# Last layer of a gated graph network: the order of h minus n, the row statistics and the moment operations on the vector engine

## The chip, the cores and the metric

The kernel runs on one core of one Trainium2 chip. The metric is the device time of one execution in microseconds (us), the median over runs. The engines are TensorE (PE in the profile), VectorE (DVE), ScalarE (ACT), GpSimd (POOL) and SyncE (SP), which here only issues transfers.

## The reference

50,000 nodes with 128 features each go through four layers of a gated graph convolution, then through a residual sum and a layer normalisation over each row. The graph has 75,000 directed edges (25,000 drawn ones and a loop on every node).

```
for l in range(4):
    m = x @ weight[l]
    agg = segment_sum(m[src], dst)
    gi = agg @ w_ih.T + b_ih ;  gh = x @ w_hh.T + b_hh      # three parts each: r, z, n
    r = sigmoid(i_r + h_r) ;  z = sigmoid(i_z + h_z) ;  n = tanh(i_n + r * h_n)
    x = (1 - z) * n + z * x                                 # = n + z * (x - n)
y = x + 2 * node_embed
out = (y - mean(y)) / sqrt(var(y) + 1e-5)                   # by row
```

## The kernel before

The nodes are cut into 100 blocks of 500. A block is held transposed, 128 features by 500 nodes, and products are split into high and low parts for precision. Each layer is a loop over blocks in which every engine has its own instruction stream in a hand-written order; waits on semaphores tie the streams together. The loop body is unrolled over ten blocks (`UNROLL`), so a position `u` runs from 0 to 9, and buffers are used in rings of five (`RING`).

In step b of a layer the vector engine does, for block b unless another is named:

- `r_times_hn` (L1363): `narg` = (h_n + bias) * r. It waits for `rg`, the sigmoid that ScalarE makes (L1055).
- `renew` = `new_state` of block b-1 (L1389).
- `n_argument` (L1370): adds the i_n product. ScalarE's tanh (L1059) waits for it.
- `aggregate` of block b+2 (L1344). ScalarE's rounding to the high part `a_hi` (L1042) waits for it.
- last layer only: `remainder` = `residual` of block b-2 (L1398), then `row_stats` of block b-2 (L1405): four batch-norm statistics instructions of 128 columns that read the rows that the residual has just written, behind a wait for it (L1403).
- `difference` (L1374): h minus n, behind a wait for the tanh.
- `low_part` of block b+2 (L1335).
- `product` (L1380): z times the difference. TensorE's next z product and GpSimd's next low part of h wait for it.

Small operations on 125 x 20 values normalise five blocks at once, in two positions of each ten. `half` is set at u = 2 and 7: there `moments` (three operations, L1410 to L1412) stands ahead of `difference`, `squared_difference` (L1416) behind it, and `variance` (L1422) behind `product`. The moments read the statistics of blocks b-7 to b-3, finished a step before. GpSimd's `root` (L658) waits for the variance at u = 3 and 8, and at u = 4 and 9 `shift` (L1428) on the vector engine waits for the root and stands between `r_times_hn` and the new state.

ScalarE's order in a step of the last layer is: `rg` (L1055), high part of h (L1025), first half of the output rows of block b-9 (L1077), tanh, `a_hi` of block b+2, z gate (L1063), widening of the selection (L1037), second half of the output rows, and then `rg` of the next step.

GpSimd's order is: low part of h (L652) for block b+3, `root` where there is one, and three gathers (L675) for block b+5. SyncE loads and stores in an order of its own; its load of columns for block b+5 waits for `difference`, and its load of x rows waits for the residual.

Of the kernel before, what the change touches and what calls it, by code (L numbers as in the profile page):

```python
# [31 lines left out]
RING = 5  # L32
# [17 lines left out]
ROWLAG = 2  # L50
# [25 lines left out]
def build(nc, x, src, dst, weight, w_ih, w_hh, b_ih, b_hh, out):  # L76
# [26 lines left out]
    with ctx:  # L103
# [264 lines left out]
        def after(i, u, k=1):  # L368

            i, u = i + (u + k) // UNROLL, (u + k) % UNROLL  # L370
            return UNROLL * i + u, u, i
# [10 lines left out]
        def halved(l):  # L382

            return 0 < l < L - 1
# [29 lines left out]
        def half_done(i, u, at):  # L414

            if u % RING != at % RING:
                return None
            first = u - at
            hi, hu = i + first // UNROLL, first % UNROLL
            if isinstance(hi, int) and hi < 0:  # L420
                return None
            return slice(hu, hu + RING), turn(hi, hu)
# [765 lines left out]
        def _(dve):  # L1188
# [170 lines left out]
            def r_times_hn(l, b, u):  # L1359
                g = l * NB + b  # L1360
                dve.wait_ge(s_HN, g + 1)
                dve.wait_ge(s_r, g + 1)
                v.scalar_tensor_tensor(narg[:, :], pHN[:, 0:COLS], bhh[:, 2:3], rg[:, :],  # L1363
                                       ALU.add, ALU.mult).then_inc(s_t1, 1)
# [66 lines left out]
            def fast_path():  # L1431
                for l in range(L):
                    final = l == L - 1

                    def renew(b, u, i):

                        g = l * NB + b
                        t = turn(i, u)
                        again = not (isinstance(t, int) and t == 0 and l == 0)
                        new_state(l, b, u, (TURNS * l + t if not final else TURNS * l) if again else None,  # L1440
                                  g - RING + 1 if again else None)

                    def remainder(b, u, i):
                        later = not (isinstance(i, int) and i == 0)
                        residual(b, u, u % RING, TURNS + turn(i, u) + 1, l * NB + b - UNROLL + 1 if later else None)

                    def step(i, u, first, last):
                        b = UNROLL * i + u
                        if first:
                            if l == 0:  # L1450
                                for j in range(TILES):
                                    select(1, 1, j)
                            first_aggregate(l, 0, l == 0)
                            first_low_part(l, 0)
                            first_aggregate(l, 1, l == 0)
                            first_low_part(l, 1)
                            first_aggregate(l, 2, l == 0)
                            first_low_part(l, 2)
                            if l == 0:
                                for c in range(2, RAMP):  # L1460
                                    for j in range(TILES):
                                        select(c, c, j)

                        added = final and exists_before(i, u, ROWLAG)
                        half = half_done(i, u, RING + ROWLAG) if final else None
                        shifted = half_done(i, u, OUTLAG) if final else None
                        ramp = isinstance(i, int) and i == 0 and u < RAMP
                        if last:
                            renew(*after(i, u, -1))
                        if ramp and u:  # L1470
                            renew(*after(i, u, -1))
                        if ramp and u == 3:
                            aggregate(l, 4, 4)
                        r_times_hn(l, b, u)
                        if shifted:
                            shift(*shifted)
                        if not ramp and not last:
                            renew(*after(i, u, -1))
                        n_argument(l, b, u)
                        if ramp and u == 3:  # L1480
                            low_part(l, 4, 4)
                        summed = after(i, u, 1 if ramp else 2)[:2] if exists(i, u, 2) else None
                        if summed and not (ramp and u == 3):
                            aggregate(l, *summed)
                        if added and not ramp:
                            remainder(*after(i, u, -ROWLAG))
                            row_stats(*after(i, u, -ROWLAG)[:2])
                        if half:
                            moments(*half, RING * (half[1] + 1))
                        if l == 0 and exists(i, u, RAMP) and not ramp:  # L1490
                            for j in range(TILES):
                                select(*after(i, u, RAMP)[:2], j)
                        difference(l, b, u)
                        if half:
                            squared_difference(*half)
                        if not opening(i) and exists(i, u, 3) and not final:
                            low_gathered(l, *after(i, u, 3)[:2])
                        coming = on_from(l, i, u, PRE)
                        coming = coming if coming and halved(coming[0]) else None
                        if coming and not ramp and not last:  # L1500
                            low_h(*coming[:3])
                        if summed and not (ramp and u == 3):
                            low_part(l, *summed)
                        if ramp and u == 3:
                            aggregate(l, 5, 5)
                        product(l, b, u)
                        if coming and ramp:
                            low_h(*coming[:3])
                        if half:
                            variance(*half)  # L1510
                        if ramp and u == 3:
                            low_part(l, 5, 5)
                        if opening(i) and not unsplit(l, b + 3):
                            low_gathered(l, *after(i, u, 3)[:2])
                        if added and ramp:
                            remainder(*after(i, u, -ROWLAG))
                            row_stats(*after(i, u, -ROWLAG)[:2])
                        if l == 0 and ramp:
                            for j in range(TILES):
                                select(RAMP + u, RAMP + u, j)  # L1520
                        if last:
                            renew(b, u, i)
                            if coming:
                                low_h(*coming[:3])

                    blocks(dve, step)
                    if final:
                        def last_rows(k):
                            u = UNROLL - k

                            dve.wait_ge(s_nmr, turn(GROUPS - 1, u) + (1 if k > LATE else 2))
                            for c in range(RPP // 2, RPP):
                                row = y_rows[:, u, c * D:(c + 1) * D]
                                last = v.tensor_scalar(row, row, rstd[:, u, c:c + 1], nmr[:, u, c:c + 1], ALU.mult, ALU.add)
                            last.then_inc(s_olast, 1)

                        ahead = slice(RING, UNROLL - LATE), TURNS - 1
                        late = slice(UNROLL - LATE, UNROLL), TURNS
                        moments(*ahead, NB - LATE)
                        squared_difference(*ahead)  # L1540
                        variance(*ahead)
                        for k in range(LATE, 0, -1):
                            remainder(NB - k, UNROLL - k, GROUPS - 1)
                            row_stats(NB - k, UNROLL - k)
                        shift(*ahead)
                        moments(*late, NB)
                        squared_difference(*late)
                        variance(*late)
                        for k in range(RING, LATE, -1):
                            last_rows(k)  # L1550
                        shift(*late)
                        for k in range(LATE, 0, -1):
                            last_rows(k)
# [79 lines left out]
```

## Time and profile before

| | us |
|---|---|
| median of 3 runs | 2382.85 (2382.22 to 2384.59) |
| the profiled execution, its own time | 2379.24 |
| its span, first to last instruction | 2377.3 |
| DVE busy over the span | 2185.7 (92%) |
| PE busy | 2251.5 (95%) |
| ACT busy | 1846.3 (78%) |
| POOL busy | 1747.0 (73%), a gather takes 1.04 in the mean |

All times below are of the one profiled execution. A step of the last layer is a stretch from one `r_times_hn` to the next. Instructions on VectorE and ScalarE overlap in the records: the next one starts a little before the end of the one ahead, so what a step consists of is the distances from start to start, not the durations.

### The profile page before, as it was taken

The page shows a single profiled execution, that of the slowest core. Times are in us where ns is not written, and L with a number is a line of the kernel's source. Part 1 is how long each engine was busy: PE and PEld are TensorE (multiplying, and loading weights), DVE is VectorE, ACT ScalarE, POOL GpSimd, SP SyncE. Part 2 cuts the span into 40 slices and gives each one's busy share as a digit, 9 for nine tenths or more (in the row PEclk, how much of TensorE's full clock was granted, in tenths as well). Part 3 has the DMA queues.
Part 4 walks back from the last instruction along what each step waited for, and adds up shares of the span by engine and source line. Part 5 has one row for each costly group of instructions (what it writes and reads, how often), then busy time and mean ns, then how long its engine had stood idle before and what let it go on. Part 6 is the DMA issues. An engine that isn't in the chain of part 4 may idle for free.

```text
span 2377.3 us, 49608 instructions
## 1 busy us (share of the span) xinstructions
PE 2251.5 (95%) x11728; PEld 1904.3 (80%) x11728; DVE 2185.7 (92%) x4408; ACT 1846.3 (78%) x3483; POOL 1747.0 (73%) x1654
## 2 busy tenths in 40 slices
PE   3899999999989999999979999999989999999996
PEld 2788888888868888888868888888877877777885
DVE  7699999999869999999959999999969999999998
ACT  1588888888758888888847888888856888888887
POOL 3778888888477777777647777777747888888884
PEclk7899999999999999999989999999999999999998
DMA  2355555555535555555535555555543555555553
GB/s 57 98 154 161 160 157 159 159 161 157 151 110 167 171 167 170 171 172 169 170 100 168 172 171 167 172 166 172 171 140 101 155 155 159 153 152 156 157 156 116
DMA packets 277063, 362.44 MB, mean 152 GB/s; under 512 B 107754, under 2 KB 186586, under 8 KB 276980
## 3 DMA queue, kind: packets, MB, share of 16 engines
q1 hardware_dynamic: 238196, 309.20, 42.5%
q0 software_dynamic: 38784, 52.30, 9.6%
q8 instruction: 32, 0.52, 0.1%
q14 instruction: 51, 0.42, 0.1%
HBM read 208.71 MB, written 179.20 MB: 163 GB/s over the span
## 4 chain that ended last, share of the span: by engine, by line
PE 65%; DVE 18%; issue 10%; ACT 4%; another core or an unknown queue 1%; DMA 1%; DVEq 1%; ACTq 0%; POOL 0%; SPq 0%; POOLq 0%
PE pR L839 17%; PE pZ L839 17%; PE pHN L839 8%; PE pA L827 8%; PE pO L906 6%; PE pIN L839 4%; PE pA L839 4%; DVE bn L1405 3%; DVE aggT L1344 2%; DVE diff L1374 2%; DVE y_rows L1398 2%; DVE diff L1380 2%; PE pH L778 2%; DVE narg L1370 1%
## 5 line engine op out<-in xcount | busy, mean ns | idle before, releaser
L675 POOL DMA_INDIRECT gath<-state,idx x900 | 933.3, 1037 | 266.4 <-issue 255.6
L652 POOL TENSOR_TENSOR h_lo<-hT,h_hi 128x500 fp32r<-128x500 f32 (+1 forms) x400 | 376.1, 940 | 220.7 <-ACT h_hi L1025 115.0
L675 POOL DMA_INDIRECT gath<-in_x_dram,idx x300 | 347.5, 1158 | 102.3 <-issue 74.8
L1055 ACT ACTIVATE rg<-pR,bsum 128x500 f32<-128x500 f32 x400 | 269.7, 674 | 132.5 <-PE pR L839 61.2
L1363 DVE SCALAR_TENSOR_TENSOR narg<-pHN,bhh,rg 128x500 f32<-128x500 f32 x400 | 294.0, 735 | 62.9 <-ACT rg L1055 31.1
L1380 DVE TENSOR_TENSOR diff<-pZ,diff 128x500 f32<-128x500 f32 x400 | 269.0, 672 | 9.6 <-ACT pZ L1063 6.7
L1344 DVE TENSOR_TENSOR aggT<-pA,hT 128x500 f32<-128x500 f32 x396 | 265.8, 671 | 8.5 <-remote 4.9
L1335 DVE TENSOR_TENSOR a_lo<-aggT,a_hi 128x500 fp32r<-128x500 f32 x396 | 271.2, 685 | 0.8
L1037 ACT CAST sel<-sel 128x504 fp32r (+1 forms) x400 | 245.6, 615 | 30.2 <-DVE flag_i L1319 29.8
L1063 ACT ACTIVATE pZ<-pZ,bsum 128x500 f32<-128x500 f32 x400 | 256.3, 641 | 10.6 <-remote 10.4
L906 PEld LDWEIGHTS pO<-ident,newT 128*125 128x125 f32 x1400 | 202.5, 187 | 55.0 <-DVE newT L1389 16.4
L1042 ACT CAST a_hi<-aggT 128x500 fp32r<-128x500 f32 x396 | 235.8, 596 | 12.0 <-DVE aggT L1344 7.0
L1059 ACT ACTIVATE pIN<-narg,bih 128x500 f32<-128x500 f32 x200 | 136.5, 683 | 130.9 <-DVE narg L1370 79.2
L1059 ACT ACTIVATE pA<-narg,bih 128x500 f32<-128x500 f32 x200 | 136.5, 682 | 130.2 <-DVE narg L1370 71.0
L906 PE MATMUL pO<-ident,newT 128*125 128x128 f32 x1400 | 214.3, 276 | 15.3 <-DVE newT L1389 13.8
L839 PE MATMUL pZ<-a_hi,wf_hi 128*128 128x500 f32 x400 | 184.0, 460 | 15.4 <-issue 8.2
L827 PE MATMUL pA<-sel,g_lo 128*128 128x168 f32 x810 | 194.8, 275 | 0.0
L839 PE MATMUL pR<-h_hi,whh_hi 128*128 128x500 f32 x400 | 190.8, 477 | 2.7 <-ACT rg L1055 2.7
L827 PE MATMUL pA<-sel,g_hi 128*128 128x168 f32 x810 | 186.3, 264 | 1.1 <-issue 0.8
L1069 ACT COPY o_rows<-pO 125x512 f32<-125x512 f32 x300 | 175.8, 586 | 7.1 <-PE pO L906 7.1
L1025 ACT CAST h_hi<-hT 128x500 fp32r<-128x500 f32 x300 | 179.9, 600 | 0.0
L839 PE MATMUL pR<-a_hi,wf_hi 128*128 128x500 f32 x400 | 159.2, 398 | 17.1 <-DVE a_lo L1335 9.9
(205 smaller groups left out, 6404.0 us busy)
## 6 DMA issues: line engine op xcount, KB each, us to landing
columns<-newT SPq DMA_DIRECT2D x300, 250.0 KB
hT<-columns SPq DMA_DIRECT2D x300, 250.0 KB
state<-o_rows SPq DMA_DIRECT2D x300, 224.0 KB
x_rows<-in_x_dram SPq DMA_DIRECT2D x200, 224.0 KB
out_dram<-o_rows SPq DMA_DIRECT2D x91, 224.0 KB
gath<-state,idx POOLq DMA_INDIRECT x900
state<-o_rows SPq DMA_DIRECT2D x300, 26.0 KB
idx<-edge_src SPq DMA_DIRECT2D x395, 1.5 KB
```

Of the source, the lines that this page charges most:

```text
L652: nc.gpsimd.tensor_tensor(part_of(h_lo, u)[:, cols], hT[:, u % RING, cols], part_of(h_hi, u)[:, cols].bitcast(F32), ALU.subtract).then_inc ...
L675: pool.indirect_dma_start(out=gath[:, u % RING, j, :], out_offset=None, in_=states[l], in_offset=bass.IndirectOffsetOnAxis(ap=idx[:, u % R ...
L827: last = nc.tensor.matmul(to, rows, cols, start=begins, stop=ends)
L839: last = nc.tensor.matmul(bank, w, xx, start=begins and k == 0, stop=ends and k == len(passes) - 1)
L906: last = nc.tensor.transpose(bank[0:ROWS, k * D:(k + 1) * D], newT[:, u % RING, k * CP:k * CP + ROWS], ident[:, :])
L1055: nc.scalar.activation(rg[:, :], pR[:, 0:COLS], ACT.Sigmoid, bias=bsum[:, 0:1]).then_inc(s_r, 1)
L1059: nc.scalar.activation(n_bank(u), narg[:, :], ACT.Tanh, bias=bih[:, 2:3]).then_inc(s_n, 1)
L1063: nc.scalar.activation(pZ[:, 0:COLS], pZ[:, 0:COLS], ACT.Sigmoid, bias=bsum[:, 1:2]).then_inc(s_z, 1)
L1335: v.tensor_tensor(by_rows(a_lo[:, u % RING, :]), sums_of if summed else by_rows(aggT[:, :]), by_rows(a_hi[:, u % RING, :].bitcast(F32)), A ...
L1344: v.tensor_tensor(by_rows(aggT[:, :]), sums_of, by_rows(hT[:, u % RING, :]), ALU.add).then_inc(s_agg, 1)
L1363: v.scalar_tensor_tensor(narg[:, :], pHN[:, 0:COLS], bhh[:, 2:3], rg[:, :], ALU.add, ALU.mult).then_inc(s_t1, 1)
L1380: v.tensor_tensor(diff[:, :], pZ[:, 0:COLS], diff[:, :], ALU.mult).then_inc(s_e, 1)
```

## The change

Three things move in the last layer's steps; no operation is added or taken away. `difference` goes ahead of `row_stats`, directly behind `residual`. `moments` goes behind `low_part`, ahead of `product`; `squared_difference` goes behind `product`. `variance` goes into the next step, behind its `r_times_hn`, ahead of the new state.

```
+                        spread_out = half_done(i, u, RING + ROWLAG + 1) if final else None
 ...
                         r_times_hn(l, b, u)
+                        if spread_out:
+                            variance(*spread_out)
                         if shifted:
                             shift(*shifted)
 ...
                             remainder(*after(i, u, -ROWLAG))
-                            row_stats(*after(i, u, -ROWLAG)[:2])
-                        if half:
-                            moments(*half, RING * (half[1] + 1))
 ...
                         difference(l, b, u)
-                        if half:
-                            squared_difference(*half)
+                        if added and not ramp:
+                            row_stats(*after(i, u, -ROWLAG)[:2])
 ...
+                        if half:
+                            moments(*half, RING * (half[1] + 1))
                         product(l, b, u)
+                        if half:
+                            squared_difference(*half)
                         if coming and ramp:
                             low_h(*coming[:3])
-                        if half:
-                            variance(*half)
```

## Rows read from the trace of the kernel before

**Rows 1.** Windows, last layer: us, then busy us by engine (instructions), PE clock, DMA share, GB/s.
```profile
1850.00:2300.00 450.00, 439.58 (x2171) 359.15 (x2169) 447.34 (x1025) 381.64 (x775) 388.34 (x325) 1.00 0.54 155
```
**Rows 2.** Timeline, VectorE, one ordinary step: start, us, engine, line, operation, tiles.
```profile
2106.06 0.74 DVE L1363 SCALAR_TENSOR_TENSOR narg<-pHN,bhh,rg 128x500 f32<-128x500 f32 x1
...
2107.30 0.67 DVE L1370 TENSOR_TENSOR narg<-pIN,narg 128x500 f32<-128x500 f32 x1
2107.89 0.67 DVE L1344 TENSOR_TENSOR aggT<-pA,hT 128x500 f32<-128x500 f32 x1
2108.47 0.68 DVE L1398 SCALAR_TENSOR_TENSOR y_rows<-x_rows,pO 125x512 f32<-125x512 f32 x1
2109.19 0.87 DVE L1405 BATCH_NORM_STATS2 bn<-y_rows 125x6 f32<-125x128 f32 x4
2109.97 0.66 DVE L1374 TENSOR_TENSOR diff<-hT,pIN 128x500 f32<-128x500 f32 x1
2110.55 0.68 DVE L1335 TENSOR_TENSOR a_lo<-aggT,a_hi 128x500 fp32r<-128x500 f32 x1
2111.14 0.67 DVE L1380 TENSOR_TENSOR diff<-pZ,diff 128x500 f32<-128x500 f32 x1
2111.76 0.74 DVE L1363 SCALAR_TENSOR_TENSOR narg<-pHN,bhh,rg 128x500 f32<-128x500 f32 x1
```
**Rows 3.** Timeline, ScalarE, the same step.
```profile
2108.01 0.68 ACT L1059 ACTIVATE pIN<-narg,bih 128x500 f32<-128x500 f32 x1 [0.77 <-issue]
2108.62 0.60 ACT L1042 CAST a_hi<-aggT 128x500 fp32r<-128x500 f32 x1
2109.13 0.64 ACT L1063 ACTIVATE pZ<-pZ,bsum 128x500 f32<-128x500 f32 x1
...
2110.20 0.88 ACT L1077 ACTIVATE o_rows<-y_rows,nmr,rstd 125x128 f32<-125x128 f32 x2
2110.98 0.66 ACT L1055 ACTIVATE rg<-pR,bsum 128x500 f32<-128x500 f32 x1
```
**Rows 4.** Timeline, VectorE, two early steps without output rows on ScalarE.
```profile
1808.20 0.73 DVE L1363 SCALAR_TENSOR_TENSOR narg<-pHN,bhh,rg 128x500 f32<-128x500 f32 x1
...
1813.86 0.73 DVE L1363 SCALAR_TENSOR_TENSOR narg<-pHN,bhh,rg 128x500 f32<-128x500 f32 x1
```
**Rows 5.** Timeline, VectorE, the step with `half`, which starts at 2111.76.
```profile
2115.67 0.18 DVE L1410 TENSOR_TENSOR mv<-bn 125x20 f32<-125x20 f32 x1
...
2115.97 0.67 DVE L1374 TENSOR_TENSOR diff<-hT,pA 128x500 f32<-128x500 f32 x1
...
2117.84 0.19 DVE L1422 SCALAR_TENSOR_TENSOR veps<-mv 125x20 f32<-125x20 f32 x1
2117.94 0.73 DVE L1363 SCALAR_TENSOR_TENSOR narg<-pHN,bhh,rg 128x500 f32<-128x500 f32 x1
```
**Rows 6.** Timeline, ScalarE, the `rg` that ends in that step.
```profile
2116.68 0.66 ACT L1055 ACTIVATE rg<-pR,bsum 128x500 f32<-128x500 f32 x1
```
**Rows 7.** Timeline, VectorE, the shift ahead of the new state.
```profile
2124.29 0.18 DVE L1428 SCALAR_TENSOR_TENSOR nmr<-mv,rstd 125x20 f32<-125x20 f32 x1
2124.38 0.66 DVE L1389 TENSOR_TENSOR newT<-diff,pIN 128x500 f32<-128x500 f32 x1
```
**Rows 8.** Timeline, GpSimd: the first root, a later root, and two gathers behind it.
```profile
1829.15 3.58 POOL L658 TENSOR_TENSOR rstd<-veps,mhalf 125x20 f32<-125x20 f32 x1
...
2119.53 3.57 POOL L658 TENSOR_TENSOR rstd<-veps,mhalf 125x20 f32<-125x20 f32 x1
...
2124.65 1.00 POOL L675 DMA_INDIRECT gath<-state,idx  x1 [0.31 <-issue]
...
2128.42 1.36 POOL L675 DMA_INDIRECT gath<-state,idx  x1 [0.16 <-issue]
```
**Rows 9.** Waits, 1850 to 2300: who waited for whom: us in total, times, longest.
```profile
POOL gath L675 <- issue: 57.9, 225, 0.3
PEld pZ L839 <- issue: 25.7, 62, 0.8
```

## The prediction

> **What bounds the kernel now.** I read the page first, then the last layer by windows, and then one step of it engine by engine in the timeline. From 1850 to 2300 us VectorE is busy 447 of 450 us at a granted TensorE clock of 1.00 [rows 1]. That looks as if every 0.01 us saved on VectorE came off the time. The timeline of a step says otherwise.
>
> An ordinary step runs from one r times h_n to the next, 2106.06 to 2111.76, 5.70 us [rows 2]. All distances from start to start between long VectorE operations are 0.58 or 0.59, with two exceptions. One is residual to row statistics, 2108.47 to 2109.19, 0.72. The other is product to the next r times h_n, 2111.14 to 2111.76, 0.62. The second shows a wait: rg starts at 2110.98 and ends at 2111.64 [rows 3], and r times h_n starts 0.12 later. In the step with the small operations rg ends at 2117.34 [rows 6] and r times h_n starts 0.60 after it [rows 5], so there VectorE's own order was last. In the ordinary steps ScalarE was.
>
> So there is a loop over two engines, and it sets an ordinary step:
>
> - VectorE, r times h_n to aggregate (the new state and the n argument between): 2106.06 to 2107.89, 1.83, and the aggregate's 0.67 [rows 2]: 2.50
> - its end at 2108.56 to the start of a_hi at 2108.62: 0.06 [rows 3]
> - ScalarE without a pause: a_hi to z gate 0.51, z gate to output rows (the widening between) 1.07, output rows to rg 0.78, rg itself 0.66 [rows 3]: 3.02
> - rg to r times h_n: 0.12
>
> The sum is 5.70, the step as measured. VectorE's own order, had nothing held it, is 5.70 less the 0.03 by which the product's distance (0.62) exceeds the usual 0.59: 5.67. The early steps agree. There ScalarE has no output rows, and a step is 1813.86 - 1808.20 = 5.66 [rows 4]. VectorE and the loop lie 0.03 apart, and the loop is the longer.
>
> TensorE is not the bound: in those 450 us (79 steps of 5.70, or 77 with the longer ones) it waited 25.7 us ahead of the z product in the weight loads alone [rows 9], a third of a us per step. GpSimd is close: 388.3 us busy [rows 1] and 57.9 us between gathers [rows 9] are 446 of 450.
>
> **Ordinary steps, three of five.** The difference moves between the residual and the row statistics. The statistics' wait for the residual is then satisfied when they come up, and their distance falls from 0.72 to 0.59: 0.13 saved. No row shows statistics behind a difference. The bounds are 0 saved (the distance stays whatever stands ahead) and 0.15 (0.57, just under the shortest distance between long operations in this step); I take 0.13, since every long pair in the step without a fresh result has 0.58 or 0.59. VectorE's own order becomes 5.54. But statistics, difference, low part and product are none of them in the loop, which stays 5.70. What is late next is rg, as now; r times h_n then waits 0.16 longer. Value: 0. If that cover were gone (a loop as short as VectorE's order), it would be worth 0.13 per step.
>
> The difference itself comes earlier. It would start at 2108.47 + 0.59 = 2109.06; the tanh ends at 2108.69 [rows 3], 0.37 before, and rg shows 0.12 to be enough from a ScalarE end to a VectorE start. 0.25 is left. Cost 0. Queued behind it are the statistics, the low part and the product, all with slack. SyncE's load of columns waits for the difference and goes 0.9 us earlier in its queue, ahead of an output store that waits for ScalarE; the DMA share is 0.54 [rows 1], so I give it nothing.
>
> **The step with half, one in five.** It is 2117.94 - 2111.76 = 6.18 now [rows 2, 5], which is VectorE's own order: 5.67 and five small operations of about 0.10 (three moments take 0.30 from 2115.67 to 2115.97, the variance 0.10 from 2117.84 to 2117.94). The moments were already waiting for nothing new, and so was the squared difference behind a whole h minus n; the new places save no stall there. After the change: 6.18 less 0.13 for the statistics, less 0.10 for the variance that leaves the step: 5.95. That is still above the loop's 5.70, so VectorE is last and the whole 0.23 comes off the time.
>
> **The step behind it.** The variance now stands between r times h_n and the new state, inside the loop. The nearest row is the shift in the same place, 2124.29 to the new state at 2124.38: 0.09 [rows 7]; I take 0.10, the distance the variance has today; bounds 0 and 0.19, its whole duration. The step goes from 5.70 to 5.80. The step with the shift keeps its 5.79 or so.
>
> GpSimd's root waits for the variance. Now the variance ends at 2118.03 and the root starts at 2119.53 [rows 8], behind the low part of h. After, it ends at 2117.94 - 0.23 + 0.66 + 0.19 = 2118.56, with 0.97 to spare. The root ends at 2123.10 and the shift runs at 2124.29, 1.19 later. Cost 0; without that cover, each us would hold up the shift and with it the new state.
>
> **The sum.** Per five blocks: -0.23 + 0.10 = -0.13. There are 19 such groups in the steps; in the first, the root at 1829.15 to 1832.73 [rows 8] ends a moment before its shift and is behind GpSimd's gathers, so I give that group nothing. 18 x 0.13 = 2.3 us. Profiled execution: 2379.24 - 2.3 = 2376.9. The median of the runs is 3.6 above it; the same difference on the median gives 2380.5. Layers 0 to 2, the ramp and the tail behind the last step keep their order and get 0. From the bounds: 0.15 and 0 for variance give -0.25 per group, -4.5 us; 0 and 0.19 give +0.09, +1.6.
>
> A rule speaks against the step that earns this. The Trainium skill, page "VectorE: DVE Perf Modes", section "The DRAIN you can't avoid", says that chained VectorE operations took the same time with a semaphore after each as with one at the end: the semaphore costs nothing extra. The row has 0.72 against 0.59, so I take the row. By the rule the 0.13 would stay, and the sum would be 18 x (0.10 - 0.10) = 0.
>
> **The rivals.**
>
> (a) Nothing comes of it: the 0.72 belongs to the statistics, not to the wait. For it: only this one pair shows 0.72, and its first operation differs in kind from all others. Against it: the start 0.03 behind the residual's end, where all other pairs overlap. The group's sum is 0: 2382.85. The skill's rule above is this case.
>
> (b) All steps gain. The 0.12 from rg to r times h_n would be chance and VectorE the only bound. For it: 447 of 450 us busy. Against it: the same 0.12 in ordinary steps, 0.60 in the step with small operations, and 5.66 where ScalarE has less to do. Price: 0.13 x 96 blocks = 12.5 us. But GpSimd doesn't follow so far: five steps take 3 x 5.70 + 6.18 + 5.79 = 29.07 now, and the slack I can see is the one gather of 1.36 against 1.00 or so [rows 8], some 0.35. 19 x 0.35 = 6.7: 2376.2, or 2370.4 if GpSimd gives way.
>
> (c) Slower: GpSimd becomes the bound. It is occupied 446 of 450 us and has its one long gather where the low part of a step begins. The low part moves 0.13 earlier in the step, and a second gather of the fifteen per group could meet it. That is +0.35 per group on 29.07. It decides from the group in which the root's spare 1.19 is used up: 1.19 / (0.35 + 0.13), after two or three groups. 16 x 0.35 = 5.6: 2388.5. Against it: why that gather is long isn't shown, and in five steps only one is.
>
> (d) The tanh comes too late for the earlier difference. It would have to end 0.25 + 0.16 = 0.41 later than now. It has 0.77 of idle time ahead of it and starts right behind its argument. I give it little; it is in the remainder.
>
> **How the numbers follow.** Forecast 0.68, (a) 0.12, (b) 0.08, (c) 0.07, the rest 0.05, on both sides. About 0.2%, 4.8 us, is what a measurement can tell from no change. The forecast and (a) are within it. Faster by more: (b) and some of the rest, and the edge of the forecast: 0.13. Slower by more: (c) and a little: 0.07. The same: 0.80. The range from 2376.5 to 2384.6 holds the forecast with its bounds, (a) with the spread of the runs, and leaves out most of (b) and (c). The forecast's own range is 2378.3 to 2382.5.
>
> **What would show it.** Ordinary steps still 5.69 to 5.70, with rg ending 0.12 before r times h_n and product to r times h_n now about 0.75. Residual to difference and difference to statistics 0.59 each. Step with half about 5.95, the next about 5.79, 28.9 per five. A step of 5.6 or less would refute the loop. Statistics 0.72 behind the difference would confirm (a). A shift that starts right behind the root's end in every group would mean (c).

## The result, and the profile after

The changed kernel takes 2396.53 us (six runs, 2390.53 to 2398.44) against 2384.01 us for the kernel before (2382.22 to 2387.55): a ratio of 1.0043, 95% interval 1.0031 to 1.0055. By that ratio, of runs taken in turn, it is slower by about 10 us; the two medians lie 12.5 apart. The forecast was 2380.5, a little faster, with a range up to 2384.6.

The profiled execution took 2396.49 us, its span is 2394.6. All that was moved did what it should, except for one instruction, the variance. Here is VectorE's timeline of a step with half and the step behind it, in the changed kernel; it answers to [rows 2, 5].

```profile
1979.60 0.68 DVE L1398 SCALAR_TENSOR_TENSOR y_rows<-x_rows,pO 125x512 f32<-125x512 f32 x1
1980.20 0.67 DVE L1374 TENSOR_TENSOR diff<-hT,pIN 128x500 f32<-128x500 f32 x1
1980.78 0.87 DVE L1405 BATCH_NORM_STATS2 bn<-y_rows 125x6 f32<-125x128 f32 x4
...
1983.04 0.19 DVE L1416 SCALAR_TENSOR_TENSOR mv<-mv 125x20 f32<-125x20 f32 x1
1983.14 0.74 DVE L1363 SCALAR_TENSOR_TENSOR narg<-pHN,bhh,rg 128x500 f32<-128x500 f32 x1
1983.79 0.80 DVE L1422 SCALAR_TENSOR_TENSOR veps<-mv 125x20 f32<-125x20 f32 x1
1984.51 0.66 DVE L1389 TENSOR_TENSOR newT<-diff,pIN 128x500 f32<-128x500 f32 x1
...
1989.54 0.74 DVE L1363 SCALAR_TENSOR_TENSOR narg<-pHN,bhh,rg 128x500 f32<-128x500 f32 x1
```

Residual to difference is 0.60 and difference to statistics 0.58: the 0.72 of [rows 2] is gone. The step with half starts at 1977.19 (the row is in the fence after next) and ends at 1983.14: 5.95, as forecast. But the variance takes 0.80 instead of the 0.19 of [rows 5], the new state starts 0.72 behind it, and the step is 1989.54 - 1983.14 = 6.40 instead of 5.80. GpSimd's timeline at that moment shows what it ran beside:

```profile
1982.18 1.25 POOL L675 DMA_INDIRECT gath<-state,idx  x1 [0.30 <-issue]
1983.44 1.08 POOL L652 TENSOR_TENSOR h_lo<-hT,h_hi 128x500 fp32r<-128x500 f32 x1
1984.67 3.57 POOL L658 TENSOR_TENSOR rstd<-veps,mhalf 125x20 f32<-125x20 f32 x1
```

The low part of h runs from 1983.44 to 1984.52. The variance comes up at 1983.79, inside it, and ends at 1984.59, 0.07 behind its end. Only then does the new state go on, and it lies in the loop. Below, an instruction is called held when its record is longer than the same operation's elsewhere and ends with an instruction of the other engine.

The ordinary steps are 5.69, as before. VectorE and ScalarE around one of them:

```profile
1971.50 0.74 DVE L1363 SCALAR_TENSOR_TENSOR narg<-pHN,bhh,rg 128x500 f32<-128x500 f32 x1
...
1976.45 0.67 DVE L1380 TENSOR_TENSOR diff<-pZ,diff 128x500 f32<-128x500 f32 x1
1977.19 0.74 DVE L1363 SCALAR_TENSOR_TENSOR narg<-pHN,bhh,rg 128x500 f32<-128x500 f32 x1
```
```profile
1976.42 0.66 ACT L1055 ACTIVATE rg<-pR,bsum 128x500 f32<-128x500 f32 x1
```

Product to r times h_n is now 0.74, and r times h_n still starts 0.11 behind rg's end at 1977.08. VectorE gained 0.13 per step and spends it waiting for ScalarE.

Over steps 10 to 89 of the last layer (the ten first and last ones left out) five blocks take, from the starts of r times h_n in each trace, 29.05 us before and 29.51 after. 18 groups make 18 x 0.46 = 8.3 us of the 10. The spans of the two profiled executions differ by more, 17.3 us: 3.9 of it has come about before the last layer's first step, where no instruction was moved, and 5.1 in the first ten steps (71.4 against 66.3); experiment 12 looks at these.

### The profile page after: what moved, and what is told of

It reads as the page before. It is cut to its first block, busy times and chain, and to the rows that moved or that the text cites. A ratio compares the mean times of both kernels' runs of the same rounds, so it can differ in the third digit from the quotient of the medians.

```text
span 2394.6 us, 49608 instructions
## 1 busy us (share of the span) xinstructions
PE 2254.5 (94%) x11728; PEld 1900.1 (79%) x11728; DVE 2189.0 (91%) x4408; ACT 1846.3 (77%) x3483; POOL 1753.7 (73%) x1654
## 4 chain that ended last, share of the span: by engine, by line
PE 65%; DVE 19%; issue 8%; ACT 4%; another core or an unknown queue 2%; DMA 1%; DVEq 1%; POOL 0%; SPq 0%; ACTq 0%; POOLq 0%
PE pR L839 17%; PE pZ L839 16%; PE pHN L839 8%; PE pA L827 8%; PE pO L906 5%; PE pA L839 4%; PE pIN L839 4%; DVE narg L1370 3%; DVE diff L1374 2%; DVE bn L1405 2%; DVE aggT L1344 2%; DVE a_lo L1335 2%; DVE diff L1380 2%; PE pH L778 2%
## 5 line engine op out<-in xcount | busy, mean ns | idle before, releaser
L1335 DVE TENSOR_TENSOR a_lo<-aggT,a_hi 128x500 fp32r<-128x500 f32 x396 | 269.3, 680 | 0.7
```

Source lines behind the costliest of these rows:

```text
L1335: v.tensor_tensor(by_rows(a_lo[:, u % RING, :]), sums_of if summed else by_rows(aggT[:, :]), by_rows(a_hi[:, u % RING, :].bitcast(F32)), A ...
```

## The experiments

Each was timed in turn with the kernel before on one chip, and its ratio is to that. "Per five" is the mean of the sixteen groups of steps 10 to 89. The steps are those of one typical group; u is the position in a ring of five. In 2, 3, 6, 10, 11 and 12 one or two groups of the sixteen differ from it, in 3 and 12 one with a step of 7.36, which raises their mean by 0.06.

| | ratio (95%) | per five | the steps u = 0 to 4 |
|---|---|---|---|
| before | | 29.05 | 5.69, 5.69, 6.19, 5.69, 5.79 |
| changed | 1.0043 (1.0031 to 1.0055) | 29.51 | 5.69, 5.69, 5.95, 6.40, 5.79 |
| 1 swap only | 0.9985 (0.9973 to 0.9997) | 28.94 | 5.67, 5.69, 6.07, 5.68, 5.83 |
| 2 variance only | 1.0065 (1.0049 to 1.0081) | 29.77 | 5.69, 5.69, 6.09, 6.49, 5.79 |
| 3 one input | 1.0026 (1.0012 to 1.0039) | 29.56 | 5.69, 5.69, 5.95, 6.38, 5.79 |
| 4 spread | 1.0038 (1.0025 to 1.0052) | 29.70 | 5.67, 5.85, 5.74, 5.69, 6.75 |
| 5 root first | 1.0036 (1.0023 to 1.0048) | 29.61 | 5.67, 5.69, 5.96, 5.79, 6.48 |
| 6 variance later | 1.0045 (1.0031 to 1.0059) | 29.61 | 5.67, 5.69, 5.96, 6.18, 6.12 |
| 7 output rows together | 0.9991 (0.9979 to 1.0003) | 28.93 | 5.65, 5.65, 6.18, 5.67, 5.78 |
| 8 swap, rows together | 0.998 (0.9966 to 0.9993) | 28.90 | 5.53, 5.53, 6.13, 5.53, 6.16 |
| 9 PSUM input | 0.9989 (0.9979 to 1.0) | 28.91 | 5.69, 5.69, 5.95, 5.79, 5.79 |
| 10 all moved | 1.0029 (1.0018 to 1.0041) | 29.54 | 5.53, 5.85, 5.74, 6.34, 6.09 |
| 11 cheap root | 0.9957 (0.9941 to 0.9973) | 28.32 | 5.53, 5.85, 5.74, 5.63, 5.53 |
| 12 changed again | 1.004 (1.0027 to 1.0054) | 29.56 | 5.69, 5.69, 5.95, 6.39, 5.78 |

**1. Swap only.**

```
                             remainder(*after(i, u, -ROWLAG))
-                            row_stats(*after(i, u, -ROWLAG)[:2])
...
                         difference(l, b, u)
                         if half:
                             squared_difference(*half)
+                        if added and not ramp:
+                            row_stats(*after(i, u, -ROWLAG)[:2])
```

> Only the difference and the row statistics change places; moments, squared difference and variance stay where they were before. Theory P (the variance met GpSimd's low part of h in the step behind the half): nothing stalls here. Ordinary steps 5.69 to 5.70, half step 6.18 - 0.13 = 6.05, the next 5.69, so -0.13 per five blocks, some 2.3 us faster than before (0.1%). Rival Q (the early difference or the later statistics cost the time): the step behind the half or the ordinary steps stay longer than before and the kernel is slower, up to the 10 to 12 us of the whole change.

The half step is 6.07, the next 5.68: the swap by itself makes the kernel faster, by 0.11 per five blocks and 0.15% in the runs. The early difference costs nothing. The rival falls.

**2. Variance only.** What experiment 1 leaves out of the change, less the moves of the moments and the squared difference:

```
                         r_times_hn(l, b, u)
+                        if spread_out:
+                            variance(*spread_out)
...
                         product(l, b, u)
...
-                        if half:
-                            variance(*half)
```

> Only the variance moves, from behind the product into the next step, between r times h_n and the new state; all else as before. Theory P: the variance lasts 0.8 us or more instead of 0.19, since it starts inside GpSimd's low part of h and ends with it; the half step is 6.08, the next 6.4, about +0.6 per five blocks, +10 us (0.4 to 0.5% slower). Rival Q: half step 6.08 and next 5.79, sum as before, within 0.1%.

All the loss is here, and more than all: 6.09 and 6.49, +0.72 per five blocks. The variance takes 0.90 and ends with the low part:

```profile
2003.86 0.90 DVE L1422 SCALAR_TENSOR_TENSOR veps<-mv 125x20 f32<-125x20 f32 x1
```
```profile
2003.62 1.08 POOL L652 TENSOR_TENSOR h_lo<-hT,h_hi 128x500 fp32r<-128x500 f32 x1
```

The low part's end is 2004.70, the variance's 2004.76.

**3. One input.** The changed kernel with a variance that reads one tensor (it leaves the squared difference out, so the output differs):

```
-                v.scalar_tensor_tensor(veps[:, s, :], mv[:, s, :, 1], 1.0 / D, mv[:, s, :, 3],
-                                       ALU.mult, ALU.add).then_inc(s_eps, 1)
+                v.tensor_scalar(veps[:, s, :], mv[:, s, :, 1], 1.0 / D, EPS, ALU.mult, ALU.add).then_inc(s_eps, 1)
```

> The changed kernel, but the variance reads one tensor (the within-half variance) and two constants; the squared difference of the half means is left out of it, so the output differs. Theory P in the form that the stall needs a VectorE instruction with two SBUF tensor inputs: the variance takes 0.2 us, the step behind the half 5.79, five blocks 28.9, 2 to 3 us faster than before. Rival R (any small VectorE operation at that place stalls, for instance on its wait for the squared difference 0.75 us earlier, or on GpSimd whatever it reads): the step stays at 6.4 and the kernel 10 us slower than before.

The narrower form of the theory falls: with a single SBUF input the instruction still takes 0.78 and the step 6.38.

```profile
2006.39 0.78 DVE L1422 TENSOR_SCALAR veps<-mv 125x20 f32<-125x20 f32 x1
```

Its low part ran from 2006.04 to 2007.13.

**9. PSUM input.** Run later, but it is the counterpart: the same place, and the second tensor lies in PSUM (the values differ, and the second operation is a maximum instead of a sum). The added lines make L1428 the variance's line in this kernel.

```
+                v.scalar_tensor_tensor(veps[:, s, :], mv[:, s, :, 1], 1.0 / D,
+                                       n_bank(u)[0:ROWS, 0:RING * RPP].rearrange("p (r k) -> p r k", k=RPP),
+                                       ALU.mult, ALU.max).then_inc(s_eps, 1)
```

> The changed kernel, but the second tensor that the variance reads lies in PSUM (twenty columns of the tanh result) instead of SBUF, so its value is another and the output differs. In the traces so far no VectorE operation with a PSUM operand was lengthened beside GpSimd's low part, while operations with all tensors in SBUF were, even with one input. If that is the line, the variance takes 0.2 us, the step behind the half 5.79 and five blocks 28.9 to 29.2 (a later low part of the sums may still be held). If any small operation is held, 0.8 us and 6.40 again.

It takes 0.18 to 0.19, and in the early groups it does so inside a low part. VectorE and GpSimd in two of them:

```profile
1896.04 0.19 DVE L1428 SCALAR_TENSOR_TENSOR veps<-mv,pA 125x20 f32<-125x20 f32 x1
1925.01 0.18 DVE L1428 SCALAR_TENSOR_TENSOR veps<-mv,pIN 125x20 f32<-125x20 f32 x1
```
```profile
1895.70 1.08 POOL L652 TENSOR_TENSOR h_lo<-hT,h_hi 128x500 fp32r<-128x500 f32 x1
...
1924.66 1.08 POOL L652 TENSOR_TENSOR h_lo<-hT,h_hi 128x500 fp32r<-128x500 f32 x1
```

1896.04 lies 0.34 behind the low part's start, as the held variance of the changed kernel does (0.35), and it is not lengthened. From the sixth group on, the variance starts 0.01 to 0.05 ahead of the low part, so only the first five are the test. The step behind the half is 5.79 and five blocks take 28.91: the sum of the prediction, had the variance not been held.

**4. Spread.** The swap, and the small operations spread over two steps, out of the loop (the lines against the kernel before; the variance stays where it was there):

```
+                        if early:
+                            moments(*early, RING * (early[1] + 1))
+                        if half:
+                            squared_difference(*half)
                         product(l, b, u)
```

> The swap, and the small operations over two steps: moments one step earlier, between low part and product; the squared difference in the half step between low part and product; the variance behind the product as before. None of them stands between r times h_n and aggregate. From the loop of 5.70 and VectorE's own order of 5.54 in a step: 5.84 with the three moments, 5.74 with the squared difference and variance, then 5.70, 5.79 (shift) and 5.70, so 28.77 per five blocks against 29.07: 19 x 0.30 = 5.5 us faster than before (0.2%). If VectorE alone were the bound, ordinary steps would be 5.54 and the gain over 10 us. If the low parts or the small operations meet GpSimd's work in their new places, single steps exceed these values by up to 0.8 us.

Four of five steps are as worked out, 5.85, 5.74, 5.69 and 5.67. The step with the shift is 6.75. There the low part of the sums (`low_part`, L1335), on VectorE, meets the low part of h, on GpSimd:

```profile
2013.19 1.75 DVE L1335 TENSOR_TENSOR a_lo<-aggT,a_hi 128x500 fp32r<-128x500 f32 x1
```
```profile
2013.13 1.26 POOL L652 TENSOR_TENSOR h_lo<-hT,h_hi 128x500 fp32r<-128x500 f32 x1
```

1.75 is 1.10 more than its 0.65. A long operation is held as a short one is: it ends 0.55 behind the low part of h, nearly its whole own duration, as if it began only there.

**5. Root first.** The changed kernel; GpSimd's root ahead of its low part:

```
...
+                        if half:
+                            root(*half)
                         coming = on_from(l, i, u, PRE)
                         if coming:
                             split_h(*coming[:3], l * NB + b if exists_before(i, u, 1) else None)
...
-                        if half:
-                            root(*half)
```

> The changed kernel, but on GpSimd the root stands ahead of the low part of h in the steps u = 3 and 8, so no low part can run when the variance comes. Theory H (a VectorE operation whose tensors all lie in SBUF, other than the row statistics, is held while GpSimd's low part runs): the variance takes 0.2 us instead of 0.8 and the step behind the half 5.79 instead of 6.40. The low part moves to about 5 us behind r times h_n, where it can meet the next low part of the sums; then one later step is up to 0.8 us longer than in the changed kernel, and the sum stays open between 28.9 and 29.7 per five blocks. Rival R (the variance is slow at that place by itself, for instance by its wait for the squared difference): 0.8 us and 6.40 as before, whatever GpSimd does.

The variance takes 0.18 and the step 5.79. Nothing on VectorE was touched, so the place alone isn't slow, nor is the wait for the squared difference. The next low part of h lands on the low part of the sums, which takes 1.51 in the step with the shift, and 6.48 follows: the loss is paid elsewhere.

```profile
1999.10 0.18 DVE L1422 SCALAR_TENSOR_TENSOR veps<-mv 125x20 f32<-125x20 f32 x1
...
2008.70 1.51 DVE L1335 TENSOR_TENSOR a_lo<-aggT,a_hi 128x500 fp32r<-128x500 f32 x1
```
```profile
2008.38 1.28 POOL L652 TENSOR_TENSOR h_lo<-hT,h_hi 128x500 fp32r<-128x500 f32 x1
```

The same run shows the hold from the other side. Behind the root the delayed low part of h meets a low part of the sums that has begun before it or with it. There VectorE isn't held (0.65 to 0.67) and the low part of h is the longer one: 1.58 where they start together, 1.23 where VectorE's is some 0.36 ahead.

```profile
2062.14 0.66 DVE L1335 TENSOR_TENSOR a_lo<-aggT,a_hi 128x500 fp32r<-128x500 f32 x1
```
```profile
2062.15 1.58 POOL L652 TENSOR_TENSOR h_lo<-hT,h_hi 128x500 fp32r<-128x500 f32 x1
```

**6. Variance later.** The changed kernel with the variance behind `n_argument` and no longer ahead of the new state.

```
                         n_argument(l, b, u)
+                        if spread_out:
+                            variance(*spread_out)
```

> The changed kernel, but the variance stands behind the n argument, 1.8 us behind r times h_n, after GpSimd's low part has ended (1.39). Theory H: variance 0.2 us, step behind the half 5.80, half step 5.95. The root starts some 0.6 us later than in the changed kernel, GpSimd's next low part comes at about 3.8 to 5.0 of the step with the shift and holds the low part of the sums, which starts at about 4.4: that step 6.2 to 6.5 instead of 5.79. Sum 29.3 to 29.6 per five blocks, slower than before by 0.2 to 0.4%. Rival: nothing but the place of the variance mattered, then five blocks take 28.9 and the kernel is 2 to 3 us faster than before.

The sum came out, but not as expected in the first step: the low part of h was later too (it started 1.27 behind r times h_n), and the variance was still held, 0.60, for 6.18. The step with the shift was 6.12, the low part of the sums taking 1.12.

```profile
2002.41 0.60 DVE L1422 SCALAR_TENSOR_TENSOR veps<-mv 125x20 f32<-125x20 f32 x1
```
```profile
2001.86 1.08 POOL L652 TENSOR_TENSOR h_lo<-hT,h_hi 128x500 fp32r<-128x500 f32 x1
```

In one group the low part ran ahead of it, 2208.85 to 2209.94. There the variance, at 2210.01 in the same place, took 0.17.

**7. Output rows together,** on the kernel before, to test the loop.

```
                         normal(i, u, 0)
+                        normal(i, u, 1)
                         n_gate(l, b, u)
...
-                        normal(i, u, 1)
```

> The kernel before, with ScalarE's second half of the output rows put directly behind the first, ahead of the tanh; it leaves the loop over ScalarE and VectorE, which falls from 5.70 to about 4.9. Loop theory: ordinary steps fall only to VectorE's own 5.66, the half step stays 6.18, five blocks 28.9 to 29.0, within 0.1% of before. If the loop theory is wrong, nothing changes at all (5.69).

Ordinary steps are 5.65, VectorE's own order; a time difference isn't resolved (the interval holds 1). Here r times h_n starts 0.49 or more behind rg's end in every step instead of 0.11, so VectorE is last. The loop theory stands.

**8. Swap, rows together.** Experiments 1 and 7 in one.

> Difference and row statistics swapped as in the first experiment, and the output rows together ahead of the tanh. Loop theory: both limits fall, VectorE's own order is 5.54, so ordinary steps go to 5.54 to 5.6, half step 6.05; by VectorE alone 28.4 per five blocks, 10 to 12 us faster than before. If GpSimd bounds at 28.7, 6 to 7 us faster (0.3%). If its low parts meet the low parts of the sums instead, single steps are up to 0.8 us longer and eat it. If the loop theory is wrong, as the first experiment: 28.9.

Ordinary steps are 5.53, so with the loop out of the way the 0.13 per step does come off. The step with the shift grows by nearly as much as the others save, from 5.78 to 6.16: the low part of the sums is held there, 1.15 against 0.65 or so. Five blocks take 28.90 (28.93 in experiment 7), where VectorE without holds would take 28.4. Its ratio, 0.998, is the lowest but for experiment 11, which leaves the root out, but its interval overlaps those of 1, 7 and 9.

```profile
2012.66 1.15 DVE L1335 TENSOR_TENSOR a_lo<-aggT,a_hi 128x500 fp32r<-128x500 f32 x1
```
```profile
2011.99 1.28 POOL L652 TENSOR_TENSOR h_lo<-hT,h_hi 128x500 fp32r<-128x500 f32 x1
```

**10. All moved.** Experiments 4 and 8 in one, and the shift out of the loop:

```
-                        shifted = half_done(i, u, OUTLAG) if final else None
+                        shifted = half_done(i, u, RING + ROWLAG + 1) if final else None
...
                         product(l, b, u)
+                        if shifted:
+                            shift(*shifted)
```

> The swap, the output rows together ahead of the tanh, the moments one step early and the squared difference between low part and product, the variance behind the product, the shift behind the product one step earlier. By VectorE alone 5.84 + 5.74 + 5.64 + 5.53 + 5.53 = 28.3 per five blocks, 19 x 0.75 = 14 us faster than before. Theory G (GpSimd's own work of five low parts, fifteen gathers and a root of 3.57 us sets a floor near 28.9, and it shows as low parts of the sums that are held): 28.9 and 3 us faster.

Worse than either theory, 29.54: the low part of the sums is held in one step (1.22, step 6.09), and in the other (6.34) the shift waits for the root:

```profile
2022.12 0.19 DVE L1428 SCALAR_TENSOR_TENSOR nmr<-mv,rstd 125x20 f32<-125x20 f32 x1 [0.63 <-POOL rstd L658]
```

**11. Cheap root.** The kernel of experiment 10, GpSimd's power replaced by a product (the inverse root is left out, so the output differs).

```
-                nc.gpsimd.tensor_tensor(rstd[:, s, :], veps[:, s, :], mhalf[:, 0:s.stop - s.start, :],
-                                        ALU.pow).then_inc(s_rstd, 1)
+                nc.gpsimd.tensor_tensor(rstd[:, s, :], veps[:, s, :], mhalf[:, 0:s.stop - s.start, :],
+                                        ALU.mult).then_inc(s_rstd, 1)
```

> As the kernel with everything moved, but GpSimd's power of -0.5 (3.57 us) is a multiplication of the same shape; the inverse root is left out and the output differs. Theory G: GpSimd has over 3 us less per five blocks, the holds vanish and five blocks take 28.3, some 14 us faster than before. If GpSimd is no floor, the same time as with the root.

GpSimd's operation falls from 3.57 to 0.23 us, no operation on VectorE is held, and the five steps are 5.53, 5.85, 5.74, 5.63, 5.53: 28.32, the sum of VectorE's own order, against 29.54 with the root. GpSimd's pauses say the same. In steps 10 to 89 of the kernel before, the changed one and every other experiment no pause between its instructions is longer than 0.32, so it is occupied throughout; in experiment 8 its 15 gathers (15.39), five low parts (6.00), root (3.57) and these pauses (3.92) are the 28.9 by themselves. Only with the cheap root does it pause longer, 0.59 in the mean ahead of a low part of h. So GpSimd's load is what stands between 28.9 and 28.3.

```profile
2013.91 0.23 POOL L658 TENSOR_TENSOR rstd<-veps,mhalf 125x20 f32<-125x20 f32 x1
```

**12. The changed kernel again.**

> The changed kernel once more, unaltered, to see what repeats. If the cost is the held variance alone: steps 10 to 89 of the last layer again 29.51 per five blocks (8.3 us over eighteen groups against 29.05), a ratio of about 1.0035 to 1.0045, while the first ten steps, 71.4 us in the first profile against 66.3 before, differ from one execution to the next. If the first ten steps are lengthened by the change, they come out near 71 again.

29.56 per five and 1.004: the groups repeat. The first ten steps took 66.3, as before the change, not the 71.4 of the first profile of the changed kernel. That difference didn't come again, and I don't count it to the change.

One thing stays open. In one group here, and in one of experiment 3, the variance is recorded from 0.6 before the low part starts, beside a gather, and still lasts 1.76, to the low part's end (the step of 7.36). Beside gathers elsewhere it takes 0.19. What held it there before the low part began isn't shown.

## Why the prediction was wrong

**The step that failed** is "the step behind it". The prediction put the variance between r times h_n and the new state at 0.10, with bounds 0 and 0.19, its own duration, by the shift's row [rows 7]. It measured 0.71: 6.40 against the 5.69 of before. The shift is in the same place of the order, but of another step, in which GpSimd is at its gathers; there is no low part of h beside it. The prediction had the low part in that very step (it let the root stand "behind the low part of h" at 2119.53) and asked only whether the root would be late. It didn't ask what the variance would run beside. At the place given to it, 0.66 behind r times h_n, the low part of h had already begun in the trace of before: it starts at 2002.30 and ends at 2003.37 in a step that begins at 2001.73.

```profile
2002.30 1.07 POOL L652 TENSOR_TENSOR h_lo<-hT,h_hi 128x500 fp32r<-128x500 f32 x1
```

With the hold the sum is: -0.23 for the half step, +0.71 for the next, +0.48 per five blocks, 18 x 0.48 = 8.6 us. The two profiles give 0.46 and 0.51, the ratio of the runs 10 us. I leave the remaining one or two open; the executions of one kernel differ by more.

A row of the kernel before had shown it, too. In the first group, where the low part of h falls late in the step, the first of the moments lies inside it and takes 0.97 instead of 0.18:

```profile
1823.42 0.97 DVE L1410 TENSOR_TENSOR mv<-bn 125x20 f32<-125x20 f32 x1
```
```profile
1823.03 1.29 POOL L652 TENSOR_TENSOR h_lo<-hT,h_hi 128x500 fp32r<-128x500 f32 x1
```

The prediction gave that group nothing and took no bound from it.

The rule was there to be found. The Trainium skill, page "SBUF — State Buffer", section "SBUF: two separate sides", says of the port pair that VectorE and GpSimd share that it is an exclusive lock: the instruction that starts first keeps it for its whole length, and the other blocks. It names two kinds of VectorE instruction that need it, those in a mode with two ports and those with two SBUF inputs, the latter only against a GpSimd instruction that reads SBUF. The traces agree on the second kind beside the low part of h (experiments 2, 4, 6, and from the other side 5) and on its absence with one SBUF and one PSUM input (experiment 9). They don't agree for the root: it reads SBUF too, and 18 low parts of the sums, with two SBUF inputs, that began beside it in the kernel before weren't lengthened. The held single-input operation of experiment 3 (0.78) can be of the first kind by the same page of the Trainium skill, section "Who interferes with whom", which has `tensor_scalar` among the operations that can enter a mode with two ports; no run here shows which mode it ran in. The row statistics, one SBUF input too, weren't lengthened: 0.27 to 0.30 inside the low part of h in 144 records of the kernel before, as in those beside nothing.

**The other steps, in order.**

- The loop of 5.70 over VectorE and ScalarE: right. Shown by experiments 7 and 8, which take 0.78 of ScalarE's work out of it. But it is not alone: GpSimd is occupied for the whole of the 29.05 as well, not only 446 of 450, since its pauses behind each low part and root weren't counted.
- Statistics from 0.72 to 0.58 or 0.59: right, in every trace with the swap. Rival (a) is out: the same statistics start 0.03 after the residual's end when they read it at once, and 0.08 before the end of the difference when that stands between. The sentence of the Trainium skill, page "VectorE: DVE Perf Modes", section "The DRAIN you can't avoid", that the semaphore costs nothing extra doesn't hold for this pair.
- The early difference costs nothing: right (experiment 1). Half step 5.95: right. That five blocks come to 28.9 without the hold (28.91 in experiment 9) is right in number, but part of that is luck: GpSimd's own sum is 28.9 as well (experiment 11), and the prediction didn't have it.
- (b), all steps gain: wrong, ordinary steps stay 5.69.
- (c), GpSimd: the mechanism was not the one that decided, but what I said of its load was nearer than I gave it. The bound shows as a wait for a semaphore only in experiment 10. Otherwise GpSimd, occupied throughout, has its low part of h wherever its load leaves it, and in some orders that lies on an operation of VectorE that it can hold. Experiments 10 and 11, which differ in the root alone, show what the load is worth: 29.54 and 28.32.
- The long gather of 1.36 in [rows 8]: I counted it as slack of GpSimd's. It starts 0.21 behind the start of a low part of the sums (2128.21 in the same trace). In steps 10 to 89 of the kernel before, 31 gathers start beside a running low part of the sums and take 1.05 to 1.39, all others 0.99 to 1.07. In the changed kernel gathers of over 1.2 are 2.1 per five blocks instead of 1.0, with the swap alone still 1.0. So the second long gather that (c) spoke of came, but not from the earlier low part. The cause of their length wasn't tried. The Trainium skill, page "SBUF — State Buffer", section "Who interferes with whom", infers that a `tensor_tensor` leaves the pair's write interface free, which is what writing a gather's descriptors needs. The low part of the sums is a `tensor_tensor`, and the gathers beside it are longer all the same.
- Two slips that change nothing: r times h_n to the new state (0.65) and the statistics to the difference (0.78) are also not 0.58 or 0.59. And the bounds of the sum, -4.5 and +1.6 us, give 2378.4 to 2384.5, not the 2378.3 to 2382.5 named as the forecast's own range.

## What to carry to other kernels

Before an instruction is moved, read the other engine's timeline at the place where it is to go, not only its own: its duration there can be that of whatever it must wait behind, and a row of the same operation at the same place of another step is no bound. Here a VectorE operation of 0.19 us with all tensors in SBUF took 0.60 to 0.90 in most groups beside GpSimd's subtraction of 128 x 500 values; one with an operand in PSUM stayed at 0.18 to 0.19. And where a loop over two engines sets the step, a stall taken out of one of them pays only where that engine is last: the same 0.13 us was worth 0 in ordinary steps, all of itself in the half step, and all of itself again once ScalarE's part was shortened, where a hold in another step took it back (28.93 and 28.90 per five blocks).

## What was not expected of the hardware

The root, GpSimd's power over 125 x 20 values, takes 3.57 us, but holds nothing: 18 low parts of the sums that begin beside it take 0.67 to 0.68 in the kernel before, as without it. The low part of h, a subtraction of 128 x 500 values, takes 1.07 to 1.29 us and holds VectorE to its end.

The hold is shorter than the trace of before would have let one work out. There the low part of h starts 0.57 behind r times h_n in that step and ends at 2003.37. The new state, at 2002.38 there, would have waited for that end with the variance ahead of it: 0.99 more, as an estimate. In the changed kernel the low part starts 0.30 behind r times h_n, ends so much the earlier, and the step is lengthened by 0.71; in experiment 2 it starts at 0.40 and the step is lengthened by 0.80. From the third group on GpSimd waits ahead of that low part in neither kernel: it comes 0.01 to 0.03 behind a gather. Why it settles at 0.30 isn't shown: in experiment 9, without any hold, it stands at 0.30 in three groups and at 0.66 from the sixth on.
